# Two fused transformer layers on one core: norms, MLPs and queries ahead of the cross attentions split 112/336 instead of 224/224, with 74 constant products fewer

## What is computed

```python
x = _layernorm(x + _L0_attn_ref(x, ...))             # linear attention, 16 heads
x = _layernorm(x + _L0_xattn_ref(x, ctx_512, ...))   # self attention + MLP, cross attention + MLP
x = _layernorm(x + _L0_ffn_ref(x, ...))              # 6-bit quantized linear layer
x = _layernorm(x + _L1_attn_ref(x, ...))             # recurrence, memory reads, MLP
x = _layernorm(x + _L1_xattn_ref(x, ctx_512, ctx_512, ...))  # cross attention
x = _layernorm(x + _L1_ffn_ref(x, ...))              # mixture of experts
```

```python
def _mha(x, y, wq, wk, wv, li1_w, li1_b, lnx_g, lnx_b, lny_g, lny_b, ln3_g, ln3_b, li2_w, li2_b, li3_w, li3_b, causal):
    xn = _ln(x, lnx_g, lnx_b); yn = _ln(y, lny_g, lny_b)
    q, k, v = per head: xn @ wq, yn @ wk, yn @ wv
    a = jax.nn.softmax(q k^T * D ** (-0.5), axis=-1)      # causal: a = a * mask, after the softmax
    x_out = x + (a v) @ li1_w + li1_b
    h = jax.nn.gelu(_ln(x_out, ln3_g, ln3_b) @ li2_w + li2_b)
    return x_out + h @ li3_w + li3_b
x = _ln(xx, ln1_g, ln1_b)
x = x + _mha(x, x, a1_..., causal=True)
x = _ln(x, ln2_g, ln2_b)
return x + _mha(x, ee, a2_..., causal=False)              # ee is the context
```

## Time and profile before

| | |
|---|---|
| median of 3 runs | 705.72 us (705.35 to 706.83) |
| the profiled execution | 707.01 us, of which 705.2 us are the span of the trace |
| PE busy | 651.6 us (92%) |
| DVE busy | 499.2 us (71%) |
| ACT busy | 338.0 us (48%) |
| POOL busy | 340.9 us (48%) |
| mean granted clock of TensorE | 0.985 of full speed |
| the two chunk loops | 137 to 340 us and 462 to 670 us |

### The profile page before, as it was taken

How to read it: one execution, slowest core, us unless ns; L and a number is a source line. 1 busy time by engine, 2 the same in 40 slices (tenths; PEclk the granted TensorE clock), 3 DMA queues, 4 the chain that set the end, 5 groups by cost and what they waited for, 6 DMA issues and landing times.

```text
span 705.2 us, 20113 instructions
## 1 busy us (share of the span) xinstructions
PE 651.6 (92%) x8927; PEld 486.8 (69%) x8927; DVE 499.2 (71%) x815; ACT 338.0 (48%) x504; POOL 340.9 (48%) x256
## 2 busy tenths in 40 slices
PE   8898987899999999999898889789999999998997
PEld 5576775677777777777775458567777777776774
DVE  3667734788988888885474462768888889888543
ACT  2153555156546546645334317255565565564443
POOL 1351362097697697573112313046866865845500
PEclk9899999999999999999999899999999999999999
DMA  9500003000000000000040000000000000000000
GB/s 271 209 1 3 3 1 133 0 3 2 2 2 3 2 2 2 2 2 3 1 149 1 0 1 0 1 2 2 2 3 2 2 2 2 2 2 2 3 1 13
DMA packets 3506, 14.84 MB, mean 21 GB/s; under 512 B 372, under 2 KB 628, under 8 KB 3420
## 3 DMA queue, kind: packets, MB, share of 16 engines
q1 hardware_dynamic: 3420, 13.56, 5.7%
HBM read 13.33 MB, written 0.23 MB: 19 GB/s over the span
## 4 chain that ended last, share of the span: by engine, by line
PE 66%; DVE 13%; ACT 9%; POOL 7%; issue 4%; DMA 1%; POOLq 0%; DVEq 0%; ACTq 0%
PE psum L911 16%; PE psum L820 8%; PE psum L869 5%; PE psum L862 5%; DVE scratch L997 4%; PE psum L864 4%; PE psum L198 4%; POOL scratch L982 3%; PE psum L667 2%; PE psum L802 1%; PE psum L826 1%; PE psum L811 1%; POOL nrm L1079 1%; ACT scratch L942 1%; PE psum L224 1%
## 5 line engine op out<-in xcount | busy, mean ns | idle before, releaser
L982 POOL TENSOR_TENSOR scratch<-scratch 125x896 bf16<-125x896 f32 x136 | 232.4, 1721 | 132.9 <-ACT scratch L970 132.2
L970 ACT ACTIVATE scratch<-psum 125x896 f32<-125x896 f32 x192 | 173.9, 918 | 192.5 <-PE psum L911 190.7
L997 DVE TENSOR_REDUCE scratch<-psum 128x1 f32<-128x500 f32 x336 | 210.5, 672 | 16.9 <-PE psum L820 8.5
L911 PE MATMUL psum<-scratch 128*125 128x448 bf16 (+1 forms) x768 | 177.2, 355 | 4.0 <-issue 3.7
L820 PE MATMUL psum<-scratch 128*128 128x500 bf16 x336 | 126.2, 376 | 4.9 <-ACT scratch L945 3.0
L911 PEld LDWEIGHTS psum<-scratch 128*125 128x125 bf16 (+1 forms) x768 | 97.3, 136 | 34.6 <-issue 4.3
L862 PE MATMUL psum<-tok,scratch 125*128 125x65 bf16 x1344 | 109.0, 195 | 1.8 <-DVE kT L1042 1.8
L864 PE MATMUL psum<-tok,scratch 125*128 125x64 bf16 x1344 | 108.3, 192 | 0.0
L862 PEld LDWEIGHTS psum<-tok,scratch 125*128 125x128 bf16 x1344 | 95.6, 97 | 14.0 <-issue 2.6
L864 PEld LDWEIGHTS psum<-tok,scratch 125*128 125x128 bf16 x1344 | 90.3, 99 | 14.4
L198 PE MATMUL psum<-w_second 128*128 128x256 bf16 x669 | 91.1, 276 | 0.0
(11 more groups left out here) (297 smaller groups left out, 823.4 us busy)
## 6 DMA issues: line engine op xcount, KB each, us to landing
raw<-ctx_dram SPq DMA_DIRECT2D x4, 672.0 KB
w_third<-fifth_dram SPq DMA_DIRECT2D x3, 636.0 KB, 5.5
w_fourth<-fourth_dram SPq DMA_DIRECT2D x3, 566.5 KB, 6.0
w_third<-third_dram SPq DMA_DIRECT2D x2, 844.0 KB, 20.5
w_third<-third_dram SPq DMA_DIRECT2D x2, 843.5 KB, 18.7
w_first<-first_dram SPq DMA_DIRECT2D x1, 996.0 KB, 4.9
w_second<-second_dram SPq DMA_DIRECT2D x1, 834.0 KB, 6.6
w_third<-fifth_dram SPq DMA_DIRECT2D x1, 636.5 KB, 8.7
```

Source lines behind the costliest of these rows:

```text
L911: mm = nc.tensor.matmul(bank(S + f, HALF, CP), lhs[0:rows, CP * c:CP * c + CP], rhs[0:rows, HALF * f:HALF * f + HALF], start=(rows == 128) ...
L970: nc.scalar.activation(CR["p"][0:CP, n % RING, :].rearrange("p (f n) -> p f n", f=2), psum[0:CP, S:S + 2, 0:HALF], ACT.Exp).then_inc(self. ...
L982: ops.tensor_tensor(CR["pl"][0:CP, n % RING, :], CR["p"][0:CP, n % RING, :], p_high(n % RING), ALU.subtract).then_inc(done, 1)
L997: nc.vector.tensor_reduce(mxp[:, r, t:t + 1], bank(B, TB), X_AXIS, ALU.max).then_inc(self.aux_freed, 1)
```

## The change

What it does, part by part:

- **Parts.** `parts_of(k)` gives `LEAD`, 112 and 336 columns (batches 0 and 1; batches 2 to 7), for the norms and MLPs 3, 4, 5, 10 and 11. The semaphores of the norms are now one for each part. Norms 0 to 2, 6 to 9, 12 and 13 keep their halves.
- **MLP and norms interleaved.** `lead_pe` takes the place of `run_pe` and `updown_pe` in the first and the third MLP: the small part's products down and its next norm's centring product stand between the large part's products.
- **Queries.** Those of the first two batches are made apart (`lead_queries_*`, ACT and DVE two tiles each); those of the other six are four products of 336 columns behind the maxima M7, M9, M11 and M14 of batch 0 (`rest_queries_*`). The front of batch 0 (`front_pe`, `front_high_act`, `front_dve_run`) has its copies split between ACT and DVE, and the large part's last norm steps between its maxima.
- **Tokens.** The T units of batch 0 stand ahead of the large part's projection (cross1) and ahead of norm 10 (cross2). POOL splits the tokens of batch 0 before its two long memsets.
- **Context.** The squares go to a free part of `w_first`; groups 0 and 1 get their root during the self attention; group 3's square, sum and root stand in chunks 3, 5 and 8 of cross1's first batch.
- **Constant products.** The program has 704 products at `keep_warm` before and 630 after. 30 become 4 ahead of `turned(3)`, 16 become 0 ahead of `outputs(3)`, 12 become 8 ahead of M0, and those of the norms 4, 5 and 11 go, with 4 and 2 put back.

The core of the diff:

```diff
+        LEAD = (slice(0, 2 * SEQ), slice(2 * SEQ, N))
         def parts_of(k):
-            return HALVES
+            return LEAD if k in (3, 4, 5, 10, 11) else HALVES
...
-                keep_warm((6, 30)[p == 3], 7)
+                keep_warm((6, 4)[p == 3], 7)
...
-                keep_warm(WARM_D if p < PAIRS - 1 else 16, 7)
+                keep_warm(WARM_D if p < PAIRS - 1 else 0, 7)
...
+                pe.wait_ge(*ready[0])
+                ups(0, range(4))
+                pe.wait_ge(*ready[1])
+                ups(1, (0, 1))
+                downs(0, range(4))
+                ups(1, (2, 3))
+                centre()
+                downs(1, (0, 1))
+                variance()
+                downs(1, (2, 3))
...
+            def front_dve_run(self, dve, beside):
+                dve.wait_ge(self.aux_ready, 4)
+                nc.vector.tensor_copy(CR["qa", 0][0:64, HALF:2 * HALF], bank(5, HALF, 64)).then_inc(self.front_dve, 1)
+                dve.wait_ge(self.front_act, 1)
+                dve.wait_ge(self.front_dve, 1)
+                nc.vector.tensor_copy(CR["qa", 0][64:128, 0:2 * HALF], CR["qa", 0][0:64, 0:2 * HALF]
+                                      ).then_inc(self.front_dve, 1)
+                self.front_low_dve(dve, 0)
+                for k, u in enumerate(FRONT[4:]):
+                    if u == ("M", 5):
+                        beside()
+                    if u == ("A", 0):
+                        self.front_low_dve(dve, 1)
+                    self.dve_unit(dve, u, k + 4, 0)
...
+                    if self is cross1 and n == 3:
+                        context_square(act, 3)
+                    if self is cross1 and n == 8:
+                        context_rstd(act, 1)
...
+                    if self is cross1 and n == 5:
+                        context_var(dve, 3)
...
+            cross1.front_pe(pe, q2_act, q2_dve, {
+                ("Q", 1): [lambda: cen_pe(pe, 5, 1, xa, both(ln_b, "xb"))], ("M", 1): [lambda: var_pe(pe, 5, 1)],
+                ("M", 7): [rest(0)], ("M", 9): [rest(1)], ("M", 11): [rest(2)], ("M", 14): [rest(3)]})
```

More of the change, by code:

```diff
@@ L767, in freed, with home @@
             def freed(self, idx):
-                return sum(u[0] not in "TN" for u, _ in self.order[:idx + 1])
+                return sum(u[0] not in "TN" and (u[0], b) != ("Q", 0) for u, b in self.order[:idx + 1])
+            def home(self, idx):
+                kind, k = self.order[idx][0]
+                if idx >= len(FRONT):
+                    return SIDE[idx % 3]
+                return 4 + k if kind in "TQ" else (0, 6, 4)[(idx - 4) % 3]
             def wait_freed(self, eng, idx):
@@ L1098, in run_pool @@
                             pool.wait_ge(self.pv_done, CHUNKS * b)
+                        if self is cross1 and b == 2:
+                            pool.wait_ge(cx_rstd, 2)
                         self.split_tokens(pool, b + 2, c - 1)
```

391 lines of the change are left out of this document (256 added, 135 removed).

## The result

| | before | after |
|---|---|---|
| time, median (lowest to highest) | 705.54 us (704.58 to 706.83) | 698.17 us (696.46 to 698.56) |
| profiled execution, time and span | 707.01 us, 705.2 us | 698.01 us, 696.2 us |
| mean granted clock of TensorE | 0.985 | 0.984 |

The ratio of after to before is 0.989, with a 95% interval of 0.9868 to 0.9911. The kernel became 7.4 us faster; 12.3 us were forecast. The two profiled executions lie 9.0 us apart.

What follows compares the result with a forecast made beforehand. Ahead of the cross attentions it took latency, then VectorE in batch 0's maxima, as the bound. Cross1's 6.9 us and cross2's 5.4 us gave 12.3 us gain, so 693.4 us, range 688.0 to 700.0 us.

Steps and rivals of the forecast that it cites:

- class of 3 to 9 us: Rival: the maxima or the chunks give more of the gain back, about 699 us; chance 0.22.
- that of 9 to 16: Likeliest case: gain of 9 to 16 us, with 693.4 us as the likeliest time; chance 0.62.
- Part 3: Maxima of batch 0: loss 2.2 us in cross1, 2.0 in cross2, plus 0.2 and 0.4 for the second low half.
- Part 4: Context sum of group 3 moved into chunk 5 of batch 0, where VectorE has no slack: loss 1.5 us.
- part 6: GpSimd's key-weight scaling moved behind the context norm, beside VectorE's norm step at 46 us: loss 0.3 us, up to 2.1.
- part 5: Cross2, front up to its first maximum, by a small chain with one norm: gain 7.8 us.
- Part 1: End of the self attention, constant products cut: last outputs end at about 87.9 us, gain 4.6 us.
- Part 2: Last outputs to first maximum of cross1, small part carried through first: 29.6 us becomes 23.1, gain 6.5 us.
- second low half: Stands behind batch 0's maxima instead of ahead, partly beside small products of A: loss 0.2 and 0.4 us.
- The rival of the clock: TensorE runs through the maxima at half clock, making the kernel 7 us slower, 713 us; chance of slower 0.05.
- The step of over 2 us: Sign of being wrong: the second VectorE step of the norm at 46 us takes over 2 us.

Runs made afterwards that it cites:

- Taking this lock away: Changed kernel with GpSimd starting cross2's tokens and the carry product only after the quantized layer's last VectorE step: 692.75 us, ratio 0.9824 to before.
- the last kernel of the experiments: Changed kernel with both GpSimd waits, no constant products ahead of five maximum products, 30 more in the memory block: 688.7 us, ratio 0.9767 to before.
- the cut alone: Kernel before with only the self attention's end constant products cut, 30 to 4 and 16 to none: 704.6 us, ratio 0.9981.
- the wait alone: Kernel before with GpSimd starting cross2's tokens only after the quantized layer's last VectorE step: 703.72 us, ratio 0.9984.
- the key wait: Changed kernel with GpSimd scaling the key weights only behind VectorE's second step of the norm at 46 us; alone: 696.58 us, ratio 0.9859 to before.

## Why the prediction was right, and where it was not

**The time is in the range, by another way than the likeliest.** The 7.4 us of the medians lie in the class of 3 to 9 us (chance 0.22), not in that of 9 to 16 (0.62), and 698.2 us is close to the 699 of that class. But what the class was made of, maxima and chunks that give more back, did not happen: parts 3 and 4 cost 4.6 us where 6.3 were forecast. The profiles put the shortfall elsewhere: 1.5 us more than forecast in part 6, 2.8 in a lock that no part names, 2.0 in part 5 and 2.7 in half clock at two other places. That these landed near 699 us is luck.

**Right in its steps.** Part 1 forecast 4.6 us and gained 4.53; the last outputs end at 88.40 us ("near 88"). Part 2 forecast 6.5 and gained 6.93, with the first maximum at 111.09 us ("near 111"). Part 3 forecast 2.2 and 2.0 us of loss in the maxima, and 2.54 and 1.60 came, with VectorE waiting for TensorE where it was said. Its second low half, 0.2 and 0.4 us, cost nothing in cross2: from the end of these maxima to that of the next it is 25.75 us, and 25.76 before. The rival of the clock, with the maxima at half clock, did not happen: from 111.09 to 126.05 us the granted clock is 1.00, and none of the half clock lies within the maxima of cross2.

**Part 6, mis-sized.** "I take 0.3 us of loss; if GpSimd comes first it is up to 2.1 us." GpSimd came first, by 0.22 us, and the loss was 1.76 us. The step of over 2 us was on the prediction's own list of what would show it wrong, and it came. GpSimd's start was left to chance although both starts were in the trace: its context norm ends at 45.55 us before and VectorE's step began at 46.56, so GpSimd was free ahead of it. The Trainium skill's page "SBUF — State Buffer", section "SBUF: two separate sides", has the shared port pair as an exclusive lock for the whole instruction. The runs agree: 2.10 us beside a 2.19 us instruction, and 0.34 us with the wait.

**A lock that no part names.** "The chunk loops and all other blocks stay as they are" failed at 363 us. A lock of the same kind cost 2.8 us there, since the fifth pack lands 1.2 us sooner against VectorE's work (GpSimd starts 2.15 us behind the start of L1288, as against 3.34 behind that of L1154, the same step before). The prediction looked at GpSimd only where the diff moves it. Taking this lock away gained 6.2 us by the medians, of which the trace shows 3.6 at this place.

**Part 5, mis-sized by the clock.** "TensorE ran at 0.57 of its clock from 424 to 428 us; ScalarE's load hides that now." It did not. TensorE ran at half clock from 414.9 to 421.7 us. Its products there are on the path, and ScalarE waited 0.92 us for the large part's product up at 425.01 us. It cost 2.0 of the 7.8 us, and with the clock full, in the last kernel of the experiments, the forecast is met to 0.1 us.

**Part 4, mis-sized.** 1.5 us were taken, and 0.49 came together with the second low half. The earlier trace rows was read as "VectorE has no slack there", but 10.10 / 15 = 0.67 us for a maximum is more than the 0.59 that VectorE needs in the earlier trace rows. The maxima were waiting for TensorE in part, although no gap shows it: TensorE started three of their products in every 2.05 us (L820 at 150.79, 152.84 and 154.88 us), 0.68 us for one. With the sum ahead of them products stand ready, and the 15 need 9.30 us.

**Half clock elsewhere.** From 340 to 344 us and from 684 to 688 us the changed kernel ran at 0.59 and 0.57, where before was at 1.00. The two cost 0.97 and 1.70 us. The first belongs to neither kernel: it is in both profiles of the changed one and not in those of before, but also in two built on before (with the cut alone and with the wait alone), and in none of the five kernels with the key wait. The second is in all profiles built on the changed kernel but one (with the key wait alone the last layers take 59.9 us, as before, in place of 61.6) and in none built on before. Why the clock falls there in the one and not in the other was not settled.

## What to carry to other kernels

When a change moves or speeds up anything on GpSimd, or lets a transfer land sooner for which GpSimd waits, list its long instructions and see which VectorE step stands beside each: at both places here the one that came first held the other to its end. A wait that puts the long GpSimd instruction behind the short VectorE step cost nothing here, where GpSimd had slack, and took away a race that hung on where a transfer lands. And a row of VectorE instructions without gaps in the trace is not proof that VectorE is full: divide its length by its count and compare with the same instruction where it runs faster.

## What the runs showed of the hardware

A packet of an instruction queue within a 2.6 MB transfer (3.8 to 5.8 us behind its first issue) goes with a last piece that lands 8.5 to 9.0 us behind its issue, as against 7.4 to 8.0 us where the packet falls at the end of the transfer or behind it (8.0 us and later). Taking 42 products out of a program at 83 us moved that packet by some 2.6 us against the transfer at 355 us, and so decided a race between GpSimd and VectorE there.

A VectorE step of 112x512 float32 takes 0.69 us alone, 1.26 us beside GpSimd's split of tokens, and 3.54 us behind the start of a carry product of 3.50 us. That product takes 3.17 us with no VectorE step beside it.

Half clock within the maxima of cross2 made them 13.85 us instead of 12.41 (the kernel before with the wait). Half clock from 414.9 to 421.7 us, ahead of them, cost 2.0 us over 54 products.
